# Routing stages without scatters: the slot table summed up on TensorE from one-hot rows and columns, unrolled, with GpSimd and ScalarE taking over the norm

## What is computed

```python
gate = softmax(xr @ Wg)                    # 16384 tokens x 16 experts
idx = argmax(gate, axis=1); gates_s = gate[idx]
onehot = one_hot(idx, E)
loc = sum((cumsum(onehot, axis=0) - 1) * onehot, axis=1)   # place of the token in its expert
valid = loc < C                            # C = 1024 slots per expert
dispatched = zeros((E, C + 1, d)).at[idx, min(loc, C)].set(xr)
h = relu(einsum('ecm,emf->ecf', dispatched[:, :C], w1)); expert_out = einsum('ecf,efm->ecm', h, w2)
combined = expert_out[idx, min(loc, C - 1)] * (gates_s * valid)[:, None]
```

## Time and profile before

| | us |
|---|---|
| median of 3 runs | 6328.39 (6325.46 to 6330.52) |
| the profiled execution | 6368.31 |
| its span, first to last instruction | 6366.6 |
| window attention, 0 to 851 | 851 |
| routing 1, 851 to 1213 | 362 |
| experts 1, 1213 to 2001 | 788 |
| projection, 2001 to 2360 | 359 |
| attention, 2360 to 5278 | 2918 |
| routing 2, 5278 to 5577 | 299 |
| experts 2, 5577 to 6366 | 789 |

### The profile page before, as it was taken

The page is one execution under the profiler, slowest core; times in us unless marked ns, Lnnn a source line. Parts: engine busy times, 40 slices in busy tenths (PEclk is TensorE's granted clock), DMA queues, the critical chain, the costliest instruction groups (busy, mean ns, idle before and its releaser), DMA issues. The chain is left out here.

```text
span 6366.6 us, 129186 instructions
## 1 busy us (share of the span) xinstructions
PE 5659.9 (89%) x49152; PEld 3922.4 (62%) x49152; DVE 4618.5 (73%) x8013; ACT 3770.5 (59%) x5534; POOL 1240.5 (19%) x1580
## 2 busy tenths in 40 slices
PE   7888855699998979999999999999999996689998
PEld 5666645599997754454445454454454545679998
DVE  7888855555655658888888888888888874455564
ACT  7888832233332436777777777777777782233332
POOL 1111113433331000011111111111111113433332
PEclk9999965699998987999999999999999996589999
DMA  1111179422223981111111111111111114222221
GB/s 46 40 40 40 43 117 151 103 97 81 84 98 120 351 300 51 53 61 62 60 61 63 61 62 60 61 63 61 62 60 61 63 44 76 44 95 95 83 84 60
DMA packets 434095, 527.83 MB, mean 83 GB/s; under 512 B 52214, under 2 KB 351892, under 8 KB 433712
## 3 DMA queue, kind: packets, MB, share of 16 engines
q1 hardware_dynamic: 400944, 457.71, 25.5%
q0 software_dynamic: 32768, 64.84, 3.3%
HBM read 337.81 MB, written 185.07 MB: 82 GB/s over the span
## 5 line engine op out<-in xcount | busy, mean ns | idle before, releaser
L1624 DVE TENSOR_REDUCE at_best<-at_psM 128x2 f32<-128x1024 f32 x2048 | 2411.2, 1220 | 380.0 <-PE at_psM L1667 379.2
L1580 ACT ACTIVATE at_p<-at_psE 128x1024 f32<-128x1024 f32 (+1 forms) x2688 | 2068.4, 819 | 613.5 <-PE at_psE L1683 579.2
L1683 PE MATMUL at_psE<-at_q,at_k 50*128 50x512 f32 x4096 | 1129.3, 429 | 84.8 <-ACT at_p L1580 83.5
L1667 PE MATMUL at_psM<-at_k,at_q 48*128 48x512 f32 x4096 | 1102.6, 456 | 51.8 <-DMA at_v<-scratch_v 30.6
L1693 PE MATMUL at_psO<-at_p,at_v 128*32 128x256 f32 x16384 | 1105.7, 388 | 0.0
L1683 PEld LDWEIGHTS at_psE<-at_q,at_k 50*128 50x128 f32 x4096 | 564.8, 187 | 485.4 <-ACT at_p L1580 232.6
L1002 ACT ACTIVATE e_h_hi<-e_psH 128x512 fp32r<-128x512 f32 x512 | 306.8, 599 | 916.0 <-PE e_psH L90 880.7
L1077 DVE SCALAR_TENSOR_TENSOR e_h_lo<-e_psH,e_h_hi 128x512 fp32r<-128x512 f32 x512 | 354.1, 692 | 596.5 <-ACT e_h_hi L1002 502.7
L1693 PEld LDWEIGHTS at_psO<-at_p,at_v 128*32 128x32 f32 x16384 | 429.4, 109 | 537.3 <-issue 314.1
L1667 PEld LDWEIGHTS at_psM<-at_k,at_q 48*128 48x128 f32 x4096 | 496.3, 188 | 361.0 <-DVE at_best L1624 170.9
L90 PE MATMUL e_psE<-e_w_hi,e_h_hi 128*128 128x256 f32 x2048 | 582.5, 284 | 0.0
(11 more groups left out here) (186 smaller groups left out, 8967.9 us busy)
## 6 DMA issues: line engine op xcount, KB each, us to landing
e_w_raw<-in_w SPq DMA_DIRECT2D x64, 1024.0 KB
scratch_qk<-cp_qkh SPq DMA_DIRECT2D x64, 512.0 KB
scratch_qk<-cp_qkl SPq DMA_DIRECT2D x64, 512.0 KB
scratch_v<-cp_va SPq DMA_DIRECT2D x32, 1024.0 KB
at_q<-scratch_qk SPq DMA_DIRECT2D x256, 128.0 KB
at_k<-scratch_qk SPq DMA_DIRECT2D x256, 128.0 KB
at_v<-scratch_v SPq DMA_DIRECT2D x128, 256.0 KB
a_x<-in_x SPq DMA_DIRECT2D x32, 512.0 KB
```

Source lines behind the costliest of these rows:

```text
L1580: nc.scalar.activation(P[:, u:u + n, :], src, ACT.Exp, scale=HD ** -0.5).then_inc(p_ready, 1)
L1624: nc.vector.reduce_max(best[j % 2][:, h, :, qt], psM[h][:], AX_X).then_inc(m_taken, 1)
L1667: last = nc.tensor.matmul(psM[h][:, a, :], Q[j][r, 128 * qt:128 * qt + 128], K[j][r, 512 * h:512 * h + 512], start=True, stop=True)
L1683: last = nc.tensor.matmul(psE[:, u - u0 if n == 2 else 2, :], K[j][r, 128 * kc:128 * kc + 128], Q[j][r, 512 * half:512 * half + 512], star ...
```

## The change

- The table is no longer scattered to HBM. For each tile POOL makes a one-hot row tile `in_row` (128 tokens x 128 rows) and an `entry` tile (128 tokens x 2 x 128 columns) that holds the token's number and its gate in the column of its slot. That is 3 POOL instructions per tile, 24 per group. PE multiplies them, 8 products per group of 256 fp32 columns each, and sums all 128 products of the stage in one PSUM tile `psTable` (`fill_table`). At the end DVE copies it into `R.index` and `R.gate` in SBUF, from which the expert stage reads. Slot `s` now lies in row `s % 128`, column `s // 128`.
- DVE's encode becomes longer by three instructions: the slot is split into row and column.
- `places` has 9 products of up to 128 columns in place of 44 of 16 columns.
- The square root is gone from ACT: POOL takes var + eps to the power -0.5 (4 small instructions per group) and ACT normalises, 8 instructions per group, with scale and bias. DVE no longer normalises. No table loads are left in the loop.
- The loop over groups is written out in full, DVE works three groups ahead, and x has 3 buffers (XO in routing 1).
- `att` is laid out so that each partition of routing 1's load is 8 KB in one piece; window attention stores it by two DMAs per group with rows of 512 bytes (it was one with rows of 1 KB). `x1` is stored as it lies in SBUF, 8 KB per partition, in a permuted order of tokens; projection then loads 4 KB per partition, attention rows of 1 KB at a step of 8 KB, and the token numbers in the table follow the new order.

The core of the diff:

```diff
-    ag = att.rearrange("(g t p) d -> g p t d", t=4, p=128)
+    ag = att.rearrange("b a (u t p) m -> u a b p t m", u=2, t=4, p=128)
...
-                sp.dma_start(row(ag, g), AT[s][:]).then_inc(att_stored[s], 16)
+                for a in range(2):
+                    sp.dma_start(row(ag[s, a], i), AT[s][:, :, 128 * a:128 * a + 128]).then_inc(att_stored[s], 16)
...
-        attg = att.rearrange("(g A c) (a m) -> g a A c m", A=64, c=16, a=2)
-        xog = x_out.rearrange("(g t p) d -> g p t d", t=TI, p=128)
+        attg = att.rearrange("b a (A c) m -> b a A (c m)", c=16)
+        xog = x_out.rearrange("(g p t) d -> g p t d", t=TI, p=128)
...
+            def inverse_deviation(q):
+                pool.wait_ge(stats_ready, q + 1)
+                after(pool, xn_ready, q - 1)
+                nc.gpsimd.tensor_scalar(minus_mean[:], mv[:, :, 0], -1.0, None, ALU.mult)
+                nc.gpsimd.tensor_scalar(var_eps[:], mv[:, :, 1], EPS, None, ALU.add).then_inc(var_ready, 1)
+                pool.wait_ge(var_ready, q + 1)
+                nc.gpsimd.tensor_tensor(rstd[q % 2][:], var_eps[:], exponent[:], ALU.pow).then_inc(rstd_ready, 1)
+                pool.wait_ge(rstd_ready, q + 1)
+                nc.gpsimd.tensor_tensor(shift[q % 2][:], minus_mean[:], rstd[q % 2][:], ALU.mult).then_inc(shift_ready, 1)
+
+            def entries(g):
+                s = g % 2
+                pool.wait_ge(codes_ready, g + 1)
+                after(pool, table_done, g - 1)
                 for t in range(TI):
-                    nc.gpsimd.indirect_dma_start(table, bass.IndirectOffsetOnAxis(ap=target_row[s][:, t:t + 1], axis=0),
-                                                 entry[s][:, t, :], None, bounds_check=E * C - 1,
-                                                 oob_is_err=False).then_inc(scattered[s], 16)
+                    nc.gpsimd.tensor_scalar(in_row[s][:, t, :], rows[:], slot_row[s][:, t:t + 1], None, ALU.is_equal)
+                    nc.gpsimd.tensor_scalar(entry[s][:, t, 0, :], columns[:], slot_column[s][:, t:t + 1], tokens[:, TI * g + t:TI * g + t + 1],
+                                            ALU.is_equal, ALU.mult)
+                    nc.gpsimd.tensor_scalar(entry[s][:, t, 1, :], columns[:], slot_column[s][:, t:t + 1], share[s][:, t:t + 1],
+                                            ALU.is_equal, ALU.mult).then_inc(entry_ready, 1)
...
+            def normalise(q):
+                act.wait_ge(shift_ready, q + 1)
+                after(act, xT_done, q - 1)
+                for t in range(TI):
+                    last = nc.scalar.activation(XN[q % 2][:, t, :], XO[q % 3][:, t, :], ACT.Identity,
+                                                bias=shift[q % 2][:, t:t + 1], scale=rstd[q % 2][:, t:t + 1])
+                last.then_inc(xn_ready, 1)
...
+            def fill_table(g):
+
+                for t in range(TI):
+                    pe.wait_ge(entry_ready, TI * g + t + 1)
+                    last = nc.tensor.matmul(psTable[:], in_row[g % 2][:, t, :], entry[g % 2][:, t, :, :],
+                                            start=g == 0 and t == 0, stop=g == NG - 1 and t == TI - 1, skip_group_check=True)
+                last.then_inc(table_done, 1)
+
+            for g in range(-1, NG + 1):
+                if here(g + 1):
+                    transposes(g + 1)
+                if here(g - 1):
+                    fill_table(g - 1)
+                if here(g):
+                    places(g)
+                if here(g + 1):
+                    logits(g + 1)
```

More of the change, by code:

```diff
@@ L543, in __init__, with routing_stage @@
         self.C = (n_tokens + self.E - 1) // self.E
[L544 to L547 removed]
+        self.columns = self.E * self.C // 128
+        self.index = ctx.enter_context(nc.sbuf_tensor("route_index", [128, self.columns], U32))
+        self.gate = ctx.enter_context(nc.sbuf_tensor("route_gate", [128, self.columns], F32))
+def routing_stage(nc, T, R, stage, x, Wg, att=None, x_out=None):
     N, D = x.shape
[L552 to L553 removed]
+    E, C, CH = R.E, R.C, R.columns
+    TI = 8
     G = 128 * TI
@@ L590, in routing_stage @@
         place = sb("place", [128, TI], F32)
-        inside = sb("inside", [128, TI], F32)
+        outside = sb("outside", [128, TI], F32)
         total = sb("total", [128, TI], F32)
         spot = sb("spot", [128, TI], F32)
-        target = sb("target", [128, TI], F32)
-        target_row = [sb(f"target_row{s}", [128, TI], U32) for s in range(2)]
-        entry = [sb(f"entry{s}", [128, TI, 2], U32) for s in range(2)]
+        slot = sb("slot", [128, TI], F32)
+        rounded = sb("rounded", [128, TI], F32)
@@ new lines, in routing_stage @@
+        slot_column = [sb(f"slot_column{s}", [128, TI], F32) for s in range(2)]
+        slot_row = [sb(f"slot_row{s}", [128, TI], F32) for s in range(2)]
+        share = [sb(f"share{s}", [128, TI], F32) for s in range(2)]
+        rows = sb("rows", [128, 128], F32)
+        columns = sb("columns", [128, CH], F32)
+        tokens = sb("tokens", [128, R.n_tiles], F32)
+        in_row = [sb(f"in_row{s}", [128, TI, 128], F32) for s in range(2)]
+        entry = [sb(f"entry{s}", [128, TI, 2, CH], F32) for s in range(2)]
@@ L661, in _ @@
-            groups(pool, NG, group)
-            for s in range(2):
-                pool.wait_ge(scattered[s], 16 * TI * (NG // 2))
-        def next_is_there(g, n=1):
-            return not (isinstance(g, int) and g + n >= NG)
+            pool.wait_ge(set_up, 1)
+            def inverse_deviation(q):
[7 more added lines that the diff above has]
+                nc.gpsimd.tensor_tensor(shift[q % 2][:], minus_mean[:], rstd[q % 2][:], ALU.mult).then_inc(shift_ready, 1)
@@ L671, in _ @@
+            for g in range(-3, NG):
+                if here(g + 3):
+                    inverse_deviation(g + 3)
+                if here(g):
+                    entries(g)
         @block.scalar
         def _(act):
-            def deviation(g):
-                act.wait_ge(stats_ready, g + 1)
-                nc.scalar.activation(std[:], mv[:, :, 1], ACT.Sqrt, bias=T.eps[:]).then_inc(std_ready, 1)
-            def take_transposed(g, s):
-                act.wait_ge(xT_done, g + 1)
-                after(act, logits_done, g - 1)
-                nc.scalar.activation(xT[s][:], psT[:], ACT.Copy).then_inc(xT_ready, 1)
@@ new lines, in take_transposed @@
+            def take_transposed(q):
+                act.wait_ge(xT_done, q + 1)
+                after(act, logits_done, q - 1)
+                nc.scalar.activation(xT[q % 2][:], psT[:], ACT.Copy).then_inc(xT_ready, 1)
+            for g in range(-2, NG):
+                if here(g):
+                    act.wait_ge(below_ready, g + 1)
+                    nc.scalar.activation(expd[:], below[:], ACT.Exp).then_inc(exp_ready, 1)
+                if here(g + 1):
+                    take_transposed(g + 1)
+                if here(g + 2):
+                    normalise(g + 2)
@@ new lines, in _, with ahead @@
+            for g in range(-3, NG):
+                def ahead(*ts):
+                    for t in ts:
+                        if here(g + 3) and t < TI:
+                            measure(g + 3, t)
+                seq.start()
+                if here(g):
+                    choose(g, ahead)
+                else:
+                    ahead(*range(-1, TI))
+                if here(g + 3):
+                    gather_statistics(g + 3)
+                if here(g):
+                    encode(g)
+                    seq.check()
@@ L832, in logits, with places @@
                                                 start=k == 0, stop=k == 1)
                 last.then_inc(logits_done, 1)
-            def places(g, s):
+            def places(g):
                 pe.wait_ge(onehot_ready, g + 1)
-                after(pe, targets_ready, g - 1)
-                for t in range(TI):
-                    nc.tensor.matmul(psC[s][:, t, :], earlier[:], onehot[s][:, t, :], start=True, stop=False)
-                    for before in range(t):
-                        nc.tensor.matmul(psC[s][:, t, :], ones[:], onehot[s][:, before, :], start=False, stop=False)
-                    last = nc.tensor.matmul(psC[s][:, t, :], ones[:], counted[s][:], start=False, stop=True)
-                last.then_inc(places_done, 1)
@@ L845, in _ @@
-            transposes(0, 0)
-            logits(0, 0)
-            def group(g, s, i):
-                if next_is_there(g):
-                    transposes(g + 1, 1 - s)
-                places(g, s)
-                if next_is_there(g):
-                    logits(g + 1, 1 - s)
-            groups(pe, NG, group)
-def expert_stage(nc, T, R, stage, x, table, w1, w2):
+                after(pe, codes_ready, g)
+                nc.tensor.matmul(psC[:], earlier[:], onehot[:], start=True, stop=False, skip_group_check=True)
```

274 lines of the change are left out of this document (123 added, 151 removed).

## The result

The changed kernel took **6492.3 us** (median of 4 runs, 6486.7 to 6501.2) against 6329.5 us for the kernel before on the same chip: ratio 1.025, 95% interval 1.023 to 1.027. It is slower by 2.5%; the forecast was 6183 us, in a range from 6080 to 6265. The profiled execution spans 6498.7 us, 132 more than before's 6366.6.

A forecast was written before the change was run, and what follows sets the result against it. Routing was taken as bound by the choose-places-logits chain, then by PE at 13.5 us per group. Gains of 91.6 (routing 1), 41.5 (routing 2) and 12 (ends), together 145 us, gave 6183 us, range 6080 to 6265.

The forecast's parts named there:

- the price of POOL's operation: Routing, building in_row and entry: 0.38 us for each of 24 one-input operations, giving POOL a chain of 12.4 us.
- Rival 1: Routing: POOL becomes the bound, period 3.2 + 24 d, gain gone at d = 0.62 us per operation; chance 0.07.
- PE's sum: Routing, per group: transposes 3.65, table products 3.4, places 0.3, logits 5.2, together 12.6 us.
- The clock: PE in routing: table products at the high clock, logits half and half, clock above 0.65.
- The period without POOL: Both routing stages: 13.5 us per group, from PE's 12.6 and POOL's 12.4 at times waiting for each other.
- ACT: Routing: eight normalises per group, below 0.5 us each, 4 us in all, covered by PE's period.
- Encode: Routing, from picking the place to the last target: 1.3 us before, 1.7 with three more small steps.
- DMA in routing 1: A's 512-byte rows make its load slow; in 8 KB pieces DMA takes 153 us, 9.6 per group, hidden.
- Rival 3: A stays slow in routing 1: 17.2 us per group there, 13.5 in routing 2, 6238 us; chance 0.10.
- What bounds the kernel now: Routing before the change: chain of choose, places and logits, plus loop entry, plus a 73.8 us wait for A.
- Ends: Routing: prologues unchanged at 41 and 28 us, tails 20 us for 26.5, gain 6 us in each stage.
- Other stages at 0: Window attention, projection, attention and expert stages: no change; projection might save up to 10 us or cost 3.

The follow-up runs named there:

- experiment 3: Changed kernel with constants for the per-partition scalars in POOL's 24 operations, 6397.5 us; or with those operations at half width, 6307.3 us.
- experiment 4: Changed kernel with DVE's two-input adding of A made a one-input operation; steady period of routing 1 21.3 us, 15 periods 317.8 us.
- experiment 1: Changed kernel with all 24 in_row and entry operations per group moved from POOL to DVE; 6218.7 us, ratio 0.973 to the kernel before.
- the mixture: Changed kernel with the 8 in_row operations per group on POOL and the 16 entry operations on DVE; 6188.0 us, ratio 0.965 to the kernel before.
- experiment 7: The mixture with the layouts of attention output and x1 put back as in the kernel before; 6188.0 us in one run, ratio 0.968.
- experiment 8: Kernel before with nine-product places, 6388.3 us; also unrolled, ratio 0.998; those plus new attention-output layout, 6377.0 us; or unrolled, nine-product, without scatters, expert stages idle.

## Why the prediction was wrong, point by point

**The step that failed** is the price of POOL's operation. I took 0.38 us for each of 24, between the cast of 281 ns and 448 ns, and called the 733 ns of a row twice as wide "far above". It was 0.60 and 0.79 us, 0.72 on average in the turn shown: POOL's sum is 17.3 us for 9.1. I had priced it by the number of elements and inputs ("one input is nearer to the cast"), and had given a price above 0.62 us a chance of 0.07. The kind of operation was left out, and it is what counts: the bare compare takes 558 ns, where a cast of twice the columns takes 390 (experiment 3). The average lies just under the 733 ns that I had called far above, and the two entry operations lie over it. The sentence of the Trainium skill that I had weighed ("GPSIMD Engine Reference", section 4.1, GpSimd roughly at line rate with one input) does not hold for this operation: a tile's three take DVE 0.72 us and POOL 2.13. The casts are another matter; between 281 and 390 ns lie 128 columns, 0.85 ns each as an estimate. Its advice, VectorE for elementwise work, is borne out.

**Rival 1 came true, and its formula was nearly enough.** At d = 0.72 it gives a period of 3.2 + 17.3 = 20.5 us; measured 21.0 and 22.1. What it lacked: the way back from the last entry to the next `in_row` took 3.7 us and not 3.2, and in routing 1 POOL's rows are stretched by 1.1 us in all, most of it gone with the edit of experiment 4. `inverse_deviation` (2.6 us, with a power of 8 columns at 1.67 us) costs nothing here, as it fits into the 3.7 us. Its decision point, d = 0.62 us, lay below what came. Even in the forecast PE's 12.6 and POOL's 12.4 us were 0.2 apart, so any error of d upward went straight into the period; the chance of 0.07 did not reflect that. One thing was not tried: PE's fixed order puts the places of a group behind the table products of the group before, and they do not need them. With places first, POOL's own work, 17.3 + 2.6 = 19.9 us, would be the least period, 1.1 us under the 21.0; that is an estimate from the turn shown.

**The other steps**, judged on experiment 1, where POOL is out of the way:
- *PE's sum, 12.6 us.* Transposes 3.44, table products 3.62 (3.4 forecast), places 0.5 (0.3), logits 3.87 (5.2): 11.4 us. Right, a little high. In the changed kernel itself the products come in twos with POOL's gaps between.
- *The clock.* Forecast above 0.65. The changed kernel has 0.61 and 0.63, with PE held up by POOL; the mixture 0.73 and 0.80 in its steady stretches. One premise was read too strongly: before the rise to 0.99 that I put down to transposes, PE had also done 7.0 us of logits, and the same 3.65 us of transposes at 5293.7 us, behind 20.2 us of idle, were followed by 0.50. So the trace of before does not show that transposes alone raise the clock.
- *The period without POOL, 13.5 us.* 15.0 and 12.7 with all on DVE, 14.2 and 11.7 with rows left on POOL. Right in size; the gain forecast (145 us, ratio 0.977) is about what experiment 1 gives (0.973). That closeness is partly luck: in experiment 1 DVE carries 5.8 us of operations per group that the forecast had on POOL, and is full.
- *ACT*, 4 us for eight normalises: 4.03. Right.
- *Encode*, 1.7 us: 5478.94 to 5480.64. Right.
- *DMA in routing 1.* The wait for A went, as forecast, and the DMA share with it, but my reason was wrong: I split 329 us of DMA time by bytes and blamed the 512-byte runs. They cost no time with the scatters gone (experiment 7), and hardly any beside them (experiment 8, 319.5 us for 318.1); the scatters did it. Rival 3 had the same wrong cause.
- *What bounds the kernel now.* Places with 44 products and the loop's entry were on the path as read, but removing them alone brought 13 us (across chips) and 5.5 us and not 65 and 14: I had not asked what is late next, the landing of the scatters.
- *Ends.* Tails of 20 us were forecast and 35.7 came in both stages; before it was 26.8 each. When the last `r_mx` of routing 2 starts, POOL still has 12.2 us of the group before to do, which the forecast had left out, then 3.7 for the way back, 17.3 for the last group (9.1 forecast) and 2.4 up to the next stage's first load. Prologues grew by 1.5 and 2.7 us.
- *Other stages at 0.* Projection 362.5 us for 359.9, attention 2928.0 for 2918.4. Over the profiles here attention took 2908 to 2921 us with the old layout of x1 and 2910 to 2928 with the new one, so no effect there is shown. Projection took 358.9 to 361.9 us in the six kernels with the old layout of x1, and 361.7 to 366.9 in the eight with the new one: my 10 us did not come, and it looks like a small loss, about the 3 us that I had set against them.

The sum of what happened: 30 periods +95.5, tails +17.9, prologues +4.2, together 117.6 us in routing. The other 14.5 us of the 132 lie outside, 9.6 of them in attention, which varies by more than that between the profiles here.

## What to carry to other kernels

An operation that no row of the trace shows should be priced by a row of the same kind, and not only of the same size. Where two engines come out within a few per cent of each other, the range has to follow the dearer bound of the one whose price is not measured. Before elementwise work goes to POOL because POOL is idle, multiply it out: 24 operations of 128 columns were 17 us there and 5.8 us on DVE, and moving them turned 2.5% lost into 2.7% won, or 3.5% with a third left on POOL. And take a suspected slow transfer's neighbours out before its layout is rewritten: the busy share of DMA (0.98 in experiment 7) told nothing of who waits.

## What was not expected of the hardware

- A compare against a constant, 128 x 128 fp32, takes POOL 558 ns; with one scalar per partition 618, compare and multiply with two 816; half the width 464 and 616. Casts of 16 x 128 and 128 x 256 take 281 and 390.
- POOL's operations are stretched from 0.59 and 0.79 to as much as 0.87 and 1.06 us beside a DVE operation that reads two inputs from SBUF.
- 128 scatters of 8 bytes per partition in a routing stage cost far more than the 2.6% of DMA time of their own packets: 15 groups of routing 1 took 319.5 us with them and 183.6 without, at 132 and 227 GB/s.
